# A first expert tile planned one routing round earlier, with the next round's routing set behind its first products

## The chip, the cores and the metric

The kernel runs on one core of a Trainium2 chip. The metric is the device time of one execution in microseconds (us). Engines are named as in the profile: PE (TensorE, with PEld for its weight loads), DVE (VectorE), ACT (ScalarE), POOL (GpSimd) and SP (SyncE, which here only issues transfers).

## The reference

One graph-transformer block on 12,500 nodes of 256 features, with 212,500 edges. It ends in a layer of eight experts, of which each node uses two:

```python
xn = _layernorm(x)
x = x + gat(xn, edge_index, W, a_src, a_dst) + mix(xn, w_qkv, ..., w_fc2, b_fc2)
h = _layernorm(x)
logits = h @ gate_w + gate_b
probs = softmax(logits)
top2_vals, top2_idx = top_k(probs, 2)
cw[n, top2_idx[n]] += top2_vals[n]
for e in range(8):
    out += cw[:, e:e+1] * (gelu(h @ W1[e] + b1[e]) @ W2[e] + b2[e])
x = x + out
```

`gat` is a graph attention over the edges with eight heads of 32 features, `mix` a linear attention with an MLP of 768. Everything is float32. Each expert is 256 to 512 to 256.

## The kernel before

The program runs in stages with a barrier between them: the nodes (to 205 us of the span), the edges with the mix branch beside them (to about 2,282 us), a short merge, and from about 2,298 us the experts. The change touches only the last stage.

**Two streams in the last stage.** Each engine's program there is a *routing* stream and an *expert tile* stream, woven together by `late` (L2385). Both are generators: `next` on one of them emits its instructions up to the next `yield`.

**Routing** (`route_*`, L1714 to L2047) walks over the 98 tiles of 128 nodes in 13 rounds of 8 tiles (the last has 2). A round goes, with the engine in brackets: divide the sums that the edges left and add them to x (DVE L1922 to L1933, tile `e_x`); mean and variance, tile `e_st` (DVE L216 to L1941); normalize into `e_hn`, eight activations for eight tiles (ACT L1864), and store x (ACT L1871); turn `e_hn` (PE L1817) and copy it to `e_hnt` (ACT L1882); gate product (PE L1827), copy (ACT L1887), turn back (PE L1837); softmax and the two best experts (DVE L1966 to L2006, with the exponential on ACT L1892); counts of earlier rows per expert (PE L1845, L1846); running places per expert (DVE L2012 to L2038, tile `e_row`); and then 16 scatters by POOL (L1736), two for each tile, which write the normalized rows with their node number and weights to `sorted_d` in HBM, where each expert has a region. The rounds 0, 1 and 12 scatter at once, the others during the next round. POOL also gathers the edge sums (`e_fr`, L1729) two rounds ahead, and SP loads `e_x` (L1776) two rounds ahead, at the first step of a round.

**Planning** (`plan_vector`, L2049). After a round is placed, DVE decides in 18 small instructions which new expert tiles are full: it fills `tile_row`, `expert` and `revs` for the tiles of that round and counts `planned` up. How many tiles a round plans is fixed ahead: `FULL[r]` is the number of tiles of 256 rows that are full after round r whatever the data. Before the change `FULL[0]` is set to 0, so that round 1 plans 9 tiles; `ROUND_OF[j]` is the round that plans tile j (1 for tiles 0 to 8, then 8 tiles for each round). There are 106 tiles, 97 of 256 rows and 9 of 128.

**Expert tiles** (`tile_order`, L2184). A tile j has five steps:
- `fetch` (SP L2215): waits for the plan and for all scatters up to that round, then for `x_tp` and `x_aim` of tile j-3; loads the tile's rows (`x_in`, L2226) and two biases (`x_b1c`, `x_b2c`).
- `start`: PE turns the rows (L2249), ACT copies them to `x_int` (L2286) and copies the expert's first weights to `x_w1c` (L2290); DVE takes the target rows and weights out of `x_in` (L2316 to L2319, it counts `x_aim`).
- `first`: eight products with W1 (PE L2260, 16 records in the trace), four Gelu activations (ACT L2299, the first two after half of the products).
- `second`: eight products with W2 (PE L2273, also 16 records).
- `store`: bias and weight (DVE L2328, L2332, tile `x_y`), and two scatters by POOL that add to the output (L2351).

The order is first(0), start(1), first(1), start(2), second(0), first(2), start(3), second(1) and so on, so that the products of tile j+1 cover the Gelu of tile j. An engine's instructions run in the order in which they are written. ACT needs another table for Gelu than for Exp; a table load stands before the first activation that needs it.

**What sets the weave.** `paces` (L2372) gives for each yield of the tile stream the number of routing steps that follow it. Up to the change the first of these is 350: all steps of rounds 0 and 1 and 108 of the 110 of round 2 stand before the first expert instruction, on every engine. From there 3 or 4 routing steps follow each yield, so that a round has sent its rows 12 yields before the tile stream needs them.

Of the kernel before, what the change touches and what calls it, by code (L numbers as in the profile page):

```python
# [59 lines left out]
AHEAD, NI, NW, NB = 3, 3, 4, 5  # L60
# [11 lines left out]
FULL = [max(-(-(2 * P * (f + n) - EXPERTS * (ET - 1)) // ET), 0) for f, n in zip(R_FIRST, R_TILES)]  # L72
HALF_PLACES = (2 * N_PAD + EXPERTS * (P - 1)) // P
HALVES = EXPERTS + (HALF_PLACES - EXPERTS) % 2
FULL[0], FULL[-1] = 0, (HALF_PLACES - HALVES) // 2 + HALVES
SLOTS = FULL[-1]
SUBS = [SUB] * (SLOTS - HALVES) + [1] * HALVES
LAST_FULL, LAST = SLOTS - HALVES - FULL[-2], SLOTS - FULL[-2]
# [1590 lines left out]
FIRST_ROUNDS = 2  # L1669
# [10 lines left out]
def placed(n):  # L1680

    return BOTH + LAG + 1 + n + 6
# [12 lines left out]
def at_once(r):  # L1695

    return r < FIRST_ROUNDS or r == len(ROUNDS) - 1


def round_steps(r):  # L1700
    n = R_TILES[r]
    return placed(n) + max(PLAN, 2 * n if at_once(r) else 0) + 1
# [481 lines left out]
def tile_order(first=None, start=None, second=None, store=None, fetch=None):  # L2184
    def call(step, j):
        if step:
            step(j)

    for j in range(AHEAD):
        yield ROUND_OF[j]  # L2190
        call(fetch, j)
    call(start, 0)
    for j in range(SLOTS + 1):
        now = ROUND_OF[min(j + 1, SLOTS - 1)]
        if j < SLOTS:
            call(first, j)
            yield now
        if j + 1 < SLOTS:
            call(start, j + 1)
            yield now  # L2200
        if j + AHEAD < SLOTS:
            yield ROUND_OF[j + AHEAD]
            call(fetch, j + AHEAD)
        if j:
            call(second, j - 1)
            yield now
            call(store, j - 1)
# [7 lines left out]
def experts_sync(sp, S, B):  # L2215
    def fetch(j):
        r, u, w, b = ROUND_OF[j], j % NI, j % NW, j % NB
        sp.wait_ge(S.planned, planned_by(j))
        at = sp.value_load(B.tile_row[0:1, j:j + 1], min_val=0, max_val=ZERO_ROWS)
        sp.wait_ge(S.e_z, 16 * (EXPERTS + 1) if r == len(ROUNDS) - 1 else 16)  # L2220
        for q in range(max(r - NH + 1, 0), r + 1):
            sp.wait_ge(S.e_g[q % NH], sent_to(q))
        if j >= NI:
            sp.wait_ge(S.x_tp, j - NI + 1)
            sp.wait_ge(S.x_aim, j - NI + 1)
        sp.dma_start(B.gin[u][:, 0:SUBS[j], :], B.sorted_d[bass.ds(at, SUBS[j] * P), :].rearrange("(t p) d -> p t d", p=P)).then_inc(S.x_in[u], 16)  # L2226

        ex = sp.value_load(B.expert[0:1, j:j + 1], min_val=0, max_val=EXPERTS - 1)
        if j >= NW:
            sp.wait_ge(S.x_h, HT * (j - NW + 1))  # L2230
        sp.wait_ge(S.x_b, 16)
        sp.dma_start(B.b1c[w][:, :], B.b1[:, bass.ds(ex, 1), :]).then_inc(S.x_wc[w], 16)
        if j >= NB:
            sp.wait_ge(S.x_st, 2 * (j - NB + 1))
        sp.dma_start(B.b2c[b][:, :], B.a["L0_ffn_b2"][bass.ds(ex, 1), :].to_broadcast([P, D])).then_inc(S.x_bc[b], 16)

    return tile_order(fetch=fetch)


def experts_tensor(pe, S, B):  # L2240
# [23 lines left out]
    def second(j):  # L2264
# [10 lines left out]
        t.then_inc(S.x_f2, 1)  # L2275

    return tile_order(first=first, start=start, second=second)


def experts_scalar(a, S, B):  # L2280
    def start(j):
        a.wait_ge(S.x_tp, j + 1)
        if j >= 2:
            a.wait_ge(S.x_f1, 2 * (j - 1))
        n = SUBS[j] * P
        a.activation(B.gt[j % 2][:, :, 0:n], B.banks[BANK_IN][:, :].rearrange("p (k n) -> p k n", k=KD)[:, :, 0:n], ACT.Copy).then_inc(S.x_gt, 1)  # L2286
        a.wait_ge(S.planned, planned_by(j))
        ex = a.value_load(B.expert[0:1, j:j + 1], min_val=0, max_val=EXPERTS - 1)
        a.wait_ge(S.x_w1, 16 * EXPERTS)
        a.activation(B.w1c[j % 2][:, :, :], B.w1[:, bass.ds(ex, 1), :, :].rearrange("p e k n -> p (e k) n"), ACT.Copy).then_inc(S.x_wt, 1)  # L2290

    def first(j):
        u, w, n = j % 2, j % NW, SUBS[j] * P
        a.wait_ge(S.x_wc[w], 16 * (j // NW + 1))
        if j >= 2:
            a.wait_ge(S.x_f2, j - 1)
        for m in range(HT):
            a.wait_ge(S.x_f1, 2 * j + m // 2 + 1)
            a.activation(B.ht[u][:, m, 0:n], B.banks[BANKS_H[m * 2 // HT]][:, m % 2 * ET:m % 2 * ET + n], ACT.Gelu,  # L2299
                         bias=B.b1c[w][:, m:m + 1]).then_inc(S.x_h, 1)  # L2300

    return tile_order(first=first, start=start)
# [58 lines left out]
def sent_at():  # L2361

    at, step = [], 0
    for r in range(len(ROUNDS)):
        for mark in marked(r, idle(round_steps(r))):
            step += 1
            if mark is True:
                at.append(step)
    return at


def paces():  # L2372

    sent, order = sent_at(), list(tile_order())
    due = [(0, sum(round_steps(r) for r in range(FIRST_ROUNDS + 1)))]
    due += [(order.index(r) - EARLY * (1 + (r == len(ROUNDS) - 1)), sent[r]) for r in range(FIRST_ROUNDS, len(ROUNDS))]
    counts, total = [], 0
    for t in range(len(order)):
        (t0, n0), (t1, n1) = next(((a, b) for a, b in zip(due, due[1:]) if t <= b[0]), due[-2:])
        counts.append(max(n0 - (-(n1 - n0) * (t - t0) // (t1 - t0)) - total, 0))  # L2380
        total += counts[-1]
    return counts


def late(route, tiles):  # L2385

    for _, pace in zip(tiles, paces()):
        for _ in range(pace):
            next(route, None)
    for _ in route:  # L2390
        pass
# [92 lines left out]
```

## Time and profile before

| | |
|---|---|
| median of 3 runs | 3251.28 us (3249.86 to 3253.3) |
| profiled execution, its time | 3246.55 us |
| profiled execution, its span | 3245.1 us |
| PE, PEld busy | 2637.8 us (81%), 2050.0 us (63%) |
| DVE, ACT, POOL busy | 2009.3 us (62%), 1549.6 us (48%), 2233.3 us (69%) |
| expert stage, first PE work to the end | 2325.8 to 3245 us |

The page divides the span in 40 slices of 81 us; the expert stage is the last twelve of them. In a timeline a row has the start in us, the duration in us, the engine, the line, the operation with its tiles, the number of instructions merged into it, and in square brackets how long the engine sat idle before it and which instruction's end freed it. An engine that is idle and not waited for costs nothing.

### The profile page before, as it was taken

Reading aid. Unit: us, or ns where it says so; the run is one execution under the profiler, and the core shown is the slowest. Engines: PE = TensorE matmul, PEld = TensorE weight load, DVE = VectorE, ACT = ScalarE, POOL = GpSimd, SP = SyncE. Lnnn points to the kernel's source line nnn. Section 1 sums busy time; section 2 is a strip of 40 time slices with the busy share of each in tenths; the row PEclk is TensorE's granted clock in tenths of the full one; section 3 lists DMA queues with packets and bytes.
Section 4 is the critical chain, followed back from the end, with each engine's and each line's share of the span. In section 5 each row is a group of like instructions: output and inputs, shape, how many; then the busy total and the mean of one; then the engine's idle time right before and its main releaser. Section 6 shows DMA issues by size and latency. Waiting matters only on the chain.

```text
span 3245.1 us, 42095 instructions
## 1 busy us (share of the span) xinstructions
PE 2637.8 (81%) x11512; PEld 2050.0 (63%) x11512; DVE 2009.3 (62%) x5437; ACT 1549.6 (48%) x3387; POOL 2233.3 (69%) x2193
## 2 busy tenths in 40 slices
PE   8657776888888898879888887566359999999998
PEld 6535555666566665656656666344248888788887
DVE  7445566777677676767767766687554555445422
ACT  5325543555555455546555455334234445545444
POOL 0277777777777777777777777776476667776644
PEclk9879997999999999989999999777579999999999
DMA  8797766566566666666666665665766766766653
GB/s 273 241 298 211 198 174 172 162 174 178 164 172 180 171 170 173 174 177 168 170 176 171 169 174 153 162 183 133 245 208 146 152 156 155 160 140 129 130 110 62
DMA packets 397607, 561.17 MB, mean 173 GB/s; under 512 B 71881, under 2 KB 317919, under 8 KB 397194
## 3 DMA queue, kind: packets, MB, share of 16 engines
q0 software_dynamic: 123696, 298.61, 36.3%
q1 hardware_dynamic: 196441, 170.69, 18.3%
q10 hardware_dynamic: 77161, 88.52, 10.3%
q8 instruction: 99, 1.62, 0.2%
q14 instruction: 210, 1.72, 0.2%
HBM read 402.45 MB, written 169.70 MB: 176 GB/s over the span
## 4 chain that ended last, share of the span: by engine, by line
PE 63%; DMA 11%; ACT 8%; POOL 7%; issue 6%; DVE 3%; ACTq 1%; SPq 0%; POOLq 0%; DVEq 0%
PE bank L1296 21%; PE bank L2260 10%; PE bank L2273 9%; DMA rows<-table,srcix 9%; PE bank L1095 7%; POOL rows L1232 5%; PE bank L1084 5%; PE bank L1057 2%; PE bank L605 1%; PE bank L606 1%; PE bank L865 1%; ACT L1336 1%; DMA out<-x_y,x_dest 1%; PE bank L2249 1%; PE bank L1278 1%
## 5 line engine op out<-in xcount | busy, mean ns | idle before, releaser
L1232 POOL DMA_INDIRECT rows<-table,srcix x1661 | 1597.8, 962 | 506.1 <-issue 357.4
L1296 PE MATMUL bank<-rows,onehot 128*128 128x272 f32 x3328 | 922.6, 424 | 58.3 <-ACT fout L1350 52.9
L1350 ACT ACTIVATE fout<-bank 128x272 f32<-128x272 f32 x1664 | 639.9, 397 | 573.6 <-PE bank L1296 523.9
L1296 PEld LDWEIGHTS bank<-rows,onehot 128*128 128x128 f32 x3328 | 664.0, 207 | 243.2 <-ACT fout L1350 79.3
L1442 DVE TENSOR_TENSOR rows<-rows,bank 128x1024 f32<-128x1024 f32 x416 | 484.2, 1214 | 169.0 <-ACT rows L1341 168.6
L2351 POOL DMA_INDIRECT out<-x_y,x_dest x203 | 328.1, 1616 | 230.7 <-DMA out<-x_y,x_dest 177.1
L2260 PE MATMUL bank<-x_int,x_w1c 128*128 128x256 f32 (+1 forms) x1696 | 378.9, 378 | 26.0 <-issue 22.9
L2273 PE MATMUL bank<-e_w,x_ht 128*128 x1624 | 370.5, 381 | 8.9 <-issue 6.6
L2260 PEld LDWEIGHTS bank<-x_int,x_w1c 128*128 128x128 f32 x1696 | 316.2, 194 | 77.4 <-issue 35.9
L2299 ACT ACTIVATE x_ht<-bank,x_b1c 128x256 f32<-128x256 f32 (+1 forms) x424 | 172.5, 461 | 392.3 <-PE bank L2260 392.2
L2273 PEld LDWEIGHTS bank<-e_w,x_ht 128*128 128x128 f32 x1624 | 300.4, 190 | 50.6 <-issue 14.3
L1084 PE MATMUL bank<-m_hnt,fc_w 128*128 128x512 f32 (+1 forms) x600 | 287.9, 605 | 30.2 <-ACT m_hid L1200 30.2
L2328 DVE TENSOR_TENSOR x_y<-bank,x_b2c 128x512 f32<-128x512 f32 (+1 forms) x106 | 70.8, 668 | 339.5 <-PE bank L2273 338.9
L1095 PE MATMUL bank<-fc_w,m_hid 128*128 128x256 f32 x1176 | 269.3, 380 | 0.0
L1278 PE MATMUL bank<-ident,sc_e 128*128 128x128 f32 x104 | 39.2, 377 | 272.0 <-ACT sc_e L1330 268.0
L1415 DVE SCALAR_TENSOR_TENSOR g_sdm<-notself,bank 128x128 f32<-128x128 f32 x104 | 29.9, 288 | 364.9 <-PE bank L1279 364.3
L1330 ACT ACTIVATE sc_e<-rows 128x256 f32<-128x256 f32 x104 | 43.3, 416 | 431.5 <-DMA rows<-table,srcix 412.3
L1095 PEld LDWEIGHTS bank<-fc_w,m_hid 128*128 128x128 f32 x1176 | 224.8, 191 | 33.4
L1736 POOL DMA_INDIRECT sorted_d<-e_hn,e_row x196 | 194.2, 991 | 65.0 <-issue 57.9
L1407 DVE TENSOR_TENSOR onehot<-bank,loc 128x2032 f32<-128x2032 f32 x104 | 235.8, 2267 | 0.2
L1278 PEld LDWEIGHTS bank<-ident,sc_e 128*128 128x128 f32 x104 | 16.7, 161 | 312.3 <-ACT sc_e L1330 306.9
L1084 PEld LDWEIGHTS bank<-m_hnt,fc_w 128*128 128x128 f32 x600 | 118.9, 200 | 126.7 <-issue 76.0
(404 smaller groups left out, 3244.0 us busy)
## 6 DMA issues: line engine op xcount, KB each, us to landing
frag<-fout ACTq DMA_DIRECT2D x104, 544.0 KB
rows<-table,srcix POOLq DMA_INDIRECT x1661
x_in<-sorted_d SPq DMA_DIRECT2D x97, 260.0 KB, 3.4
x_b2c<-in_L_ffn_b SPq DMA_DIRECT2D x106, 128.0 KB, 3.5
frag<-in_x ACTq DMA_DIRECT2D x1, 13416.0 KB
table<-hr SPq DMA_DIRECT2D x24, 544.0 KB, 4.0
xs<-in_x SPq DMA_DIRECT2D x24, 512.0 KB, 6.4
xg<-in_x SPq DMA_DIRECT2D x24, 512.0 KB, 6.3
```

Source lines behind the costliest of these rows:

```text
L1084: t = pe.matmul(bank[own[m % 2]][:, 0:n * P], B.mw1[:, kk, m * P:(m + 1) * P], B.m_hnt[:, kk, 0:n * P], start=(kk == 0), stop=(kk == KD - 1))
L1095: t = pe.matmul(bank[own[i // 2]][:, i % 2 * D:(i % 2 + 1) * D], B.m_hid[:, m, i * P:(i + 1) * P], B.mw2[:, m, :], start=(m == 0), stop=(m ...
L1232: p.indirect_dma_start(out=B.rows[b][:, j, :], out_offset=None, in_=B.table[:, :], in_offset=bass.IndirectOffsetOnAxis(ap=B.srcix[:, col:c ...
L1296: pe.matmul(B.banks[2 + c % 3][:, 0:ROW], B.onehot[k % 2][:, j, :], B.rows[k % NR][:, j, :], start=True, stop=True).then_inc(S.sum, 1)
L1350: a.activation(B.fout[k % 2][:, j, :], B.banks[2 + c % 3][:, 0:ROW], ACT.Copy).then_inc(S.ev, 1)
L1407: v.tensor_tensor(B.onehot[b][:, :, 0:P - 1], B.banks[0][:, 2 * P:3 * P - 1].unsqueeze(1).to_broadcast([P, CB, P - 1]), B.loc[:, k * CB:(k ...
L1442: v.tensor_tensor(h, h, w.unsqueeze(3).to_broadcast([P, n, GH, GF]), ALU.mult).then_inc(S.wgh, 1)
L1736: p.indirect_dma_start(out=B.sorted_d[:, :], out_offset=bass.IndirectOffsetOnAxis(ap=B.e_row[:, j, at:at + 1], axis=0), in_=B.e_hn[r % NH] ...
L2260: t = pe.matmul(out, B.w1c[u][:, k, m * P:(m + 1) * P], B.gt[u][:, k, 0:n], start=(k == 0), stop=(k == KD - 1))
L2273: t = pe.matmul(bk[BANKS_OUT[u]][:, i * D:(i + 1) * D], B.ht[u][:, m, i * P:(i + 1) * P], B.w2[:, bass.ds(ex * HT + m, 1), :], start=(m == ...
L2299: a.activation(B.ht[u][:, m, 0:n], B.banks[BANKS_H[m * 2 // HT]][:, m % 2 * ET:m % 2 * ET + n], ACT.Gelu, bias=B.b1c[w][:, m:m + 1]).then_ ...
L2351: p.indirect_dma_start(out=B.out[:, :], out_offset=bass.IndirectOffsetOnAxis(ap=B.dest[j % (NOUT + 1)][:, i:i + 1], axis=0), in_=B.y[j % N ...
```

## The change

Three edits in the planning of the order; no instruction's form changes except the plan's widths.

```diff
-FULL[0], FULL[-1] = 0, (HALF_PLACES - HALVES) // 2 + HALVES
+FULL[-1] = (HALF_PLACES - HALVES) // 2 + HALVES
...
-    call(start, 0)
+    if first or not store:
+        call(start, 0)
     for j in range(SLOTS + 1):
         now = ROUND_OF[min(j + 1, SLOTS - 1)]
         if j < SLOTS:
             call(first, j)
             yield now
+        if j == 0 and not (first or not store):
+            call(start, 0)
         if j + 1 < SLOTS:
             call(start, j + 1)
             yield now
...
-    due = [(0, sum(round_steps(r) for r in range(FIRST_ROUNDS + 1)))]
+    due = [(AHEAD, sum(round_steps(r) for r in range(FIRST_ROUNDS + 1)))]
...
     for t in range(len(order)):
+        if t < AHEAD:
+            counts.append(max(sent[order[t]] - total, 0))
+            total += counts[-1]
+            continue
```

`FULL[0]` is now 1: round 0 plans tile 0 (18 more DVE instructions), round 1 plans 8 tiles. The routing steps that follow the first yields were 350, 4, 3, 3 and are now 121, 121, 0, 108: SP's fetch of tile 0 stands behind round 0, its fetches of tiles 1 and 2 behind round 1, and the 108 steps of round 2 stand behind start(0) and first(0) on PE and ACT. On DVE start(0) stands behind those 108 steps. Then 4 routing steps follow each yield, until from the 17th yield on both programs have emitted the same number. Lines of the new program are up to 7 higher: 3 higher in the expert steps.

PE, from the last steps of round 1's routing on (`e_` names are routing, `x_` names the expert tile):

```order
 L1845 MATMUL bank<-e_both,e_before 128x64
 L1846 MATMUL bank<-e_both,ones 128x64
+L2252 MATMUL bank<-ident,x_in 128x128 x4
+L2263 MATMUL bank<-x_int,x_w1c 128x256 x8
 L1817 MATMUL bank<-ident,e_hn 128x128 x16
 L1827 MATMUL bank<-e_hnt,e_gw 32x256 x8
```

Tile 0's turn and first products moved ahead of round 2's routing; in the old program they stand behind its L1846.

ACT, from the end of round 1's routing to tile 1, with the new program alone:

```order
L2302 ACT_TABLE_LOAD [waits x_fc1_done]
L2302 ACTIVATE x_ht<-bank,x_b1c 128x256 [waits x_wc_in0]
L2302 ACTIVATE x_ht<-bank,x_b1c 128x256 [waits x_fc1_done] x3
L1864 ACTIVATE e_hn<-e_x,e_st 128x256 [waits e_moments]
L1864 ACTIVATE e_hn<-e_x,e_st 128x256 x7
L1871 DMA out<-e_x 128x4x256 [waits e_x1_ready]
L1871 DMA out<-e_x 128x4x256
L1882 ACTIVATE e_hnt<-bank 128x512 [waits e_hn_turned,e_gated]
L1882 ACTIVATE e_hnt<-bank 128x512 [waits e_hn_turned] x3
L1887 ACTIVATE e_lgt<-bank 128x256 [waits e_gated]
L1892 ACT_TABLE_LOAD
L1892 ACTIVATE e_pr<-e_lg 128x64 [waits e_less_max]
```

The whole of round 2's normalization and gate work stands behind tile 0's four Gelus, and round 2's exponential now has a table load before it (that load waits for nothing); tile 1's Gelu has another.

DVE, at the end of the moments of round 3:

```order
 L237 SCALAR_TENSOR_TENSOR e_st<-e_st 128x8
+L2331 TENSOR_TENSOR x_y<-bank,x_b2c 128x512
+L2335 TENSOR_TENSOR x_y<-x_y,x_scale 128x512
 L240 SCALAR_TENSOR_TENSOR e_st<-e_st 128x8
 L1941 SCALAR_TENSOR_TENSOR e_st<-e_st 128x8
-L2328 TENSOR_TENSOR x_y<-bank,x_b2c 128x512
-L2332 TENSOR_TENSOR x_y<-x_y,x_scale 128x512
```

Tile 0's store pair moved from behind the last step of round 3's moments to before its last two. On ACT all eight normalizations of round 3 now stand between start(3) and first(3), where before four stood ahead of first(2)'s Gelus and four behind them. On POOL 7, 6 and 3 scatters of round 2 stand before the stores of tiles 0, 1 and 2, where 9, 5 and 2 stood.

## Rows read from the trace of the kernel before

**Rows 1.** Windows: busy us (instructions) by engine, granted clock, DMA share, GB/s

```profile
2300.00:2390.00 90.00, 19.26 (x113) 13.83 (x113) 57.07 (x235) 20.53 (x42) 64.64 (x67) 0.56 0.86 289
...
3100.00:3170.00 70.00, 70.00 (x346) 61.70 (x345) 17.50 (x50) 29.39 (x58) 33.66 (x20) 1.00 0.50 89
```

**Rows 2.** Chain of waits from round 0's scatters to tile 0

```profile
2345.86 1.01 POOL sorted_d L1736
...
2364.88 0.96 POOL sorted_d L1736
...
2385.59 2.45 DMA sorted_d<-e_hn,e_row
...
2388.28 2.99 DMA x_in<-sorted_d
...
2391.32 1.13 PE bank L2249 x4
2394.51 3.77 PE bank L2260 x8
```

**Rows 3.** Timeline of ACT

```profile
2375.49 0.60 ACT L1864 ACTIVATE e_hn<-e_x,e_st 128x256 f32<-128x256 f32 x1 [25.23 <-DVE e_st L1941]
...
2379.44 1.05 ACT L1882 ACTIVATE e_hnt<-bank 128x512 f32<-128x512 f32 x2
...
2385.32 0.26 ACT L1892 ACTIVATE e_pr<-e_lg 128x64 f32<-128x64 f32 x1 [1.30 <-DVE e_lg L1973]
...
2399.64 1.57 ACT L2299 ACTIVATE x_ht<-bank,x_b1c 128x256 f32<-128x256 f32 x4
2401.15 0.60 ACT L2286 ACTIVATE x_int<-bank 128x512 f32<-128x512 f32 x1
...
2422.95 1.09 ACT L1882 ACTIVATE e_hnt<-bank 128x512 f32<-128x512 f32 x2
...
2442.76 1.28 ACT L1892 ACT_TABLE_LOAD   x1
2444.05 0.26 ACT L1892 ACTIVATE e_pr<-e_lg 128x64 f32<-128x64 f32 x1
```

**Rows 4.** Timeline of PE

```profile
2380.16 1.55 PE L1817 MATMUL bank<-ident,e_hn 128*128 128x128 f32 x8 [0.57 <-ACT e_hnt L1882]
...
2389.99 0.63 PE L1846 MATMUL bank<-e_both,ones 128*128 128x64 f32 x2
...
2410.39 3.62 PE L2260 MATMUL bank<-x_int,x_w1c 128*128 128x256 f32 x16
...
2425.16 3.72 PE L2273 MATMUL bank<-e_w,x_ht 128*128 x16 [0.40 <-issue]
```

**Rows 5.** Timeline of DVE

```profile
2349.18 0.23 DVE L1966 TENSOR_TENSOR e_lg<-bank,e_gb 128x64 f32<-128x64 f32 x1 [3.60 <-PE bank L1837]
...
2394.55 0.16 DVE L2057 CAST pl_ci<-pl_count 128x8 int32<-128x8 f32 x1
...
2398.22 0.22 DVE L1922 TENSOR_SCALAR e_rs<-e_fr 128x32 f32<-128x32 f32 x1
...
2411.28 0.17 DVE L1941 SCALAR_TENSOR_TENSOR e_st<-e_st 128x8 f32<-128x8 f32 x1
...
2472.99 0.69 DVE L2328 TENSOR_TENSOR x_y<-bank,x_b2c 128x512 f32<-128x512 f32 x1
```

**Rows 6.** Timeline of POOL: its waits behind tiles' stores

```profile
2413.06 1.61 POOL L2351 DMA_INDIRECT out<-x_y,x_dest  x1 [3.42 <-DVE x_y L2332]
...
2466.09 1.76 POOL L2351 DMA_INDIRECT out<-x_y,x_dest  x1 [6.17 <-DMA out<-x_y,x_dest]
```

**Rows 7.** Timeline of SP: the fetch of tile 9, the first of round 2

```profile
2445.39 0.37 SPq L2226 DMA_DIRECT2D x_in<-sorted_d  x1
```

**Rows 8.** Windows of 2 us, PE alone: busy, granted clock, DMA share, GB/s

```profile
2342.00:2344.00 2.00, 2.00 (x11) 0.50 1.08 397
...
2398.00:2400.00 2.00, 2.00 (x9) 0.94 1.09 343
```

## The prediction

> **What bounds the kernel now.** I read the page's slices first, then windows over the last stage, then the chain of waits from the first scatters to the first expert tile, then each engine's timeline from 2340 to 2480 us. The windows [rows 1] show two regimes. Up to 2390 us the stage is routing alone, PE is busy 19.26 of 90 us; late in the stage PE is busy 70 of 70. So the end is set by PE's stream of tiles, and a change at the stage's start moves the end by as much as it moves that stream once it is dense. The chain [rows 2] tells what starts it: POOL scatters round 0 and round 1 back to back, 32 scatters with the first at 2345.86; the last, started at 2385.59, lands 2.45 later, SP fetches tile 0 at 2388.28, PE turns it at 2391.32 and starts its products at 2394.51. Tile 0 waits for 16 scatters of round 1 which it would not need if round 0 alone had planned it.
>
> **Plan of round 0.** 18 DVE instructions. The same 18 of round 2 ran from 2394.55 to 2398.22, 3.67 us [rows 5]. They stand before L1966 of round 1, where DVE idled 3.60 us until 2349.18. Price 0, at most 0.1; POOL is still busy with round 0's scatters then and hides that too. Round 1's plan for 8 instead of 9 tiles costs the same.
>
> **Tile 0 goes earlier.** Its fetch now waits for the 16th scatter, started at 2364.88, not the 32nd at 2385.59: 20.71 us earlier [rows 2]. Shift all of tile 0 by that: turn at 2370.6, products at 2373.8. ACT was done with tile 0's four Gelus when it took up tile 1 at 2401.15 [rows 3]; shifted, it is free at 2380.44. SP issues the `e_x` loads of round 3 behind tile 0's fetch now, at about 2370 us, and those of round 4 behind tile 2's; DVE first reads round 3's after 2398.22 [rows 5], so this is free.
>
> **Round 2 waits for that.** ACT began round 2's normalization at 2375.49 [rows 3]; it now begins at 2380.44, 4.95 late. From there to the end of L1846 at 2389.99 + 0.63 = 2390.62 [rows 4] took 15.13. The exponential on this path gets a table load of 1.28, but the load waits for nothing and ACT idled 1.30 just there [rows 3]: price 0. So the new L1846 ends at T = 2380.44 + 15.13 = 2395.6. Bounds: if PE's clock is at its upper level throughout, the turns of 1.55 take 1.06 as those of round 3 did and the pair of count products saves as much: 1.0 less. If the second half of tile 0's products runs at half clock (3.77, as the first half did [rows 2], against 3.62 for all 16 at the full one [rows 4]), ACT is free 1.7 later. So T is 2394.6 to 2397.3. In the table load the trace speaks for itself: load at 2442.76, exponential at 2444.05, nothing else between [rows 3]. The Trainium skill (ScalarE: Activation LUTs, What ACT_TABLE_LOAD costs) gives a switch a drain of about 1.38 us beside the load's 1.28, about 2.66 in all; by it T would be some 1.4 us later and the sum 1.4 us worse. The rows show no such drain, so the sum goes by them.
>
> **Tile 1 and 2 on PE.** Their rows are in by then (fetch at 2388.28 as tile 0's before). PE turns tile 1 at T + 0.1, 3.2 later (as 2391.32 to 2394.51 [rows 2]) come its products, for 3.77 + 1.8 with a clock rising half way, then a turn of 0.5 and second(0) for 3.5: first(2) starts at T + 12.7 = 2408.3, where it started at 2410.39 [rows 4]. Here the change is 2.1 us ahead. Tile 1's Gelu pays the table load that tile 0's paid before; that is within this pattern.
>
> **Round 3 takes it back.** Round 3's moments (`e_st`) end on DVE. From round 2's counts (T, before 2390.62) to L1941 at 2411.28 took 20.66 [rows 5]. Three tiles' target steps stand in that piece before and after the change, but now tile 0's store pair stands in it too, two operations of 0.69 [rows 5], 1.3 with the gap. ACT gets `e_st` 0.2 after L1941 starts: at T + 20.66 + 1.3 + 0.2 = T + 22.2 = 2417.8. ACT's order then is eight normalizations, 3.95 (2375.49 to 2379.44), four Gelus of tile 3, 1.51 (2399.64 to 2401.15), and the copy of the turned rows [rows 3]; that copy started at 2422.95 and PE's second(2) followed at 2425.16 [rows 4], 2.2 later. So second(2) starts at T + 22.2 + 3.95 + 1.5 + 2.2 = T + 29.85 = 2425.45, **0.3 us later than before**. PE alone would be there at first(2) + 3.6 + 0.5 + 3.6 + 3.6 + 1.1 + 0.5 + 1.1 = 2422.3. PE waits 3.1 us for ACT there. From second(2) on PE, ACT and DVE stand in the same order as before, and all later work is the same.
>
> **POOL and SP.** A scatter takes POOL 1.27 (15 steps from 2345.86 to 2364.88 [rows 2]). Round 2's rows are ready when its plan starts, 3.9 after its counts (2394.55 [rows 5]), so at 2399.5; 7 scatters end at 2408.4; then POOL waits for tile 0's store pair until about 2417.0, where it went on at 2413.06 after a wait of 3.42 [rows 6]. With two scatters more behind that it is 3.9 + 2.5 = 6.5 us late, which the wait of 6.17 before 2466.09 [rows 6] and shorter ones ahead of it absorb. Round 2's last scatter has nine scatters and two stores of 2 x 1.9 in front of it from 2417.0 on and lands 2.45 later, at 2438.5, before SP fetched tile 9 at 2445.39 [rows 7]. SP's fetch of tile 3 waits for tile 0's target step on DVE, at T + 7.6 (2398.22) + 0.4, and lands 3 later, at 2406.6; its turn on PE stands behind first(2), at 2412. No price for either.
>
> **Sum.** 0 for the plan, POOL and SP, +0.3 us on PE's stream, from T's bounds -0.7 to +2.0. Against the profiled execution's time of 3246.55 that is 3246.85; that execution was 4.7 below the median of 3251.28, and I forecast the median: **3251.6 us**. A measurement of this kernel can tell about 0.2% (6.5 us) from no change; the forecast lies within.
>
> **The rivals.**
> - *Faster, PE decides.* If DVE or ACT are through with round 3 three us sooner than I say, PE's own path holds: 2.9 us ahead, 3248.4. For it: the bounds of T reach 1 us that way. Against: DVE's piece of 20.66 has no idle time that the change frees. Chance 0.12.
> - *Faster, the full tile.* Were round 2's and 3's routing hidden, the end would come by what tile 0 occupied of PE's path, from 2391.32 to 2394.51 + 3.77 + 1.8 = 2400.1 [rows 2], 8.8 us: 3242.8. It needs slack that the 4.95 at ACT denies. 0.05.
> - *Slower, the clock.* PE's granted clock was 0.50 in a window with PE busy for all of it [rows 8], and rose at 2398 before. The new program has sparse routing work on PE between tile 0 and T. If the clock stays at half through first(1), second(0) and first(2), the last two take 3.5 us more each and first(1)'s second half 1.9: 8.9, less the 3.1 that PE waits anyway, 5.8 over the sum, 3257.4; with second(1) at half too, 3260.9. It decides from 3.1 us of lost speed on. Against: the old program was as sparse before 2391 and the clock rose within tile 0. 0.08. The Trainium skill (TensorE: Matmul & The Clock Gate, HAM oscillation — how this bites in real kernels) warns of such pauses between bursts of products; the window with a busy PE at 0.50 shows that it can happen here.
> - *Slower, the drain.* If a table load at this place holds ACT for a further 1.4 us after its 1.28, T and the end move with it: 3253.0. Against: the load and the exponential stand back to back [rows 3]. 0.03. (This is the page's rule on table switches from above.)
> - *Slower, the fetch.* Tile 0's rows landed 3.0 after their issue [rows 2]; each us more is one us of T, and nothing covers it. 5 us more gives 3256.6. Against: fewer transfers are queued at 2368 than at 2391. 0.03.
> - *It does not do what it says.* The order shows tile 0 moved; only if its fetch waited for round 1 all the same would T be 2416 and PE some 20 us later: 3271. 0.01.
>
> The forecast keeps 0.68.
>
> **How the numbers follow.** Faster by over 6.5 us is the full tile and a bit of the first rival: 0.06. Slower by over 6.5 is the last case and the longer half of the clock rival, with a little of the fetch: 0.07. The rest, 0.87, is within. The range 3247 to 3257 takes in the bounds of the sum, the old runs' own spread of 3.4, the first rival, and the clock and fetch cases up to their nearer halves; it leaves out the full tile and the tails, under 0.2.
>
> **What would show it.** Right: PE L2252 of tile 0 at about 2370.6; ACT's first L1864 of round 2 at about 2380.4; L1846 at about 2395; an idle time of PE of 2 to 3 us before the turns of round 3 (L1817) or second(2), freed by ACT; L2276 of tile 2 at 2425 +- 2; POOL waiting some 8 us before its first L2354. Wrong: second(2) before 2423 (round 3's chain is not the bound), or PE dense but slow between 2396 and 2410 (the clock), or L2252 of tile 0 after 2375.

## The result, and the profile after

| | before | changed |
|---|---|---|
| median of the runs, us | 3251.28 (3249.07 to 3256.8, 5 runs) | 3267.34 (3265.05 to 3270.92, 5 runs) |
| ratio, 95% interval | | 1.0054 [1.0042, 1.0066] |
| profiled execution, us | 3246.55 | 3270.92 |
| its span, us; mean granted clock | 3245.1; 0.918 | 3269.5; 0.912 |

The changed kernel is 0.54% slower, 16 us. The forecast was no change. The profiled executions are 24.4 us apart: that of the changed kernel is the slowest of its five runs, and that of the kernel before lies 2.5 us under the fastest of the five in this table. The readings below are of those 24.4 us; that the medians' 16 are the same thing in a smaller dose is likely but not shown, since one execution of each kernel was profiled. 3.0 of the 24.4 lie ahead of the last stage: the first merge step on PE (L1505) starts at 2292.39, before at 2289.37. It starts anywhere from 2285.73 to 2293.26 in five profiles of other kernels below, whose work ahead of it is the same, so these 3.0 are not the change's. They are taken off wherever the two heads are compared.

One sentence is needed for the experiments further down: in some comparisons (sets of kernels timed one after another on one chip) the whole kernel ran 15 to 17% longer, the kernel before too (3731.6 to 3790.3 us), so a ratio is always against the kernel before in the same comparison; I call these the long comparisons.

**The head went nearly as forecast.** Timeline of PE in the changed kernel, to be read against [rows 2] and [rows 4]:

```profile
2374.23 1.11 PE L2252 MATMUL bank<-ident,x_in 128*128 128x128 f32 x4 [15.19 <-DMA x_in<-sorted_d]
...
2388.44 1.94 PE L1817 MATMUL bank<-ident,e_hn 128*128 128x128 f32 x8 [1.45 <-ACT e_hnt L1882]
2391.16 1.93 PE L1827 MATMUL bank<-e_hnt,e_gw 128*32 128x256 f32 x16 [0.78 <-ACT e_hnt L1882]
...
2399.76 0.64 PE L1846 MATMUL bank<-e_both,ones 128*128 128x64 f32 x2
...
2403.10 6.06 PE L2263 MATMUL bank<-x_int,x_w1c 128*128 128x256 f32 x16 [1.86 <-issue]
...
2412.89 3.62 PE L2263 MATMUL bank<-x_int,x_w1c 128*128 128x256 f32 x16
...
2428.56 1.94 PE L1817 MATMUL bank<-ident,e_hn 128*128 128x128 f32 x8 [2.45 <-ACT e_hnt L1882]
2430.30 1.99 PE L2276 MATMUL bank<-e_w,x_ht 128*128 x5
```

Timeline of ACT, against [rows 3]:

```profile
2383.77 4.04 ACT L1864 ACTIVATE e_hn<-e_x,e_st 128x256 f32<-128x256 f32 x8
...
2393.55 1.28 ACT L1892 ACT_TABLE_LOAD   x1
2395.09 0.26 ACT L1892 ACTIVATE e_pr<-e_lg 128x64 f32<-128x64 f32 x1 [0.25 <-DVE e_lg L1973]
...
2422.45 0.60 ACT L1864 ACTIVATE e_hn<-e_x,e_st 128x256 f32<-128x256 f32 x1 [3.64 <-DVE e_st L1941]
```

Tile 0 is turned where it was forecast (2371.2 without the 3.0; 2370.6 said), round 2's counts end at 2397.4 instead of 2395.6, and the second products of tile 2 start at 2427.3 instead of 2425.45. They stood at 2425.16 before, so PE's stream is 2.1 us late.

**The loss is behind the head.** GpSimd's timeline of the changed kernel, against [rows 6]:

```profile
2404.62 0.99 POOL L1736 DMA_INDIRECT sorted_d<-e_hn,e_row  x1 [4.25 <-DVE e_hn L2038]
...
2422.40 1.61 POOL L2354 DMA_INDIRECT out<-x_y,x_dest  x1 [8.01 <-DVE x_y L2335]
...
2461.61 1.58 POOL L2354 DMA_INDIRECT out<-x_y,x_dest  x1 [2.32 <-DMA out<-x_y,x_dest]
...
2471.35 2.38 POOL L2354 DMA_INDIRECT out<-x_y,x_dest  x1 [6.30 <-DMA out<-x_y,x_dest]
...
2478.22 1.54 POOL L2354 DMA_INDIRECT out<-x_y,x_dest  x1 [2.63 <-DMA out<-x_y,x_dest]
```

POOL stands idle for 8.01 us before tile 0's pair of output scatters, as forecast. But the wait of 6.17 that was to absorb the delay [rows 6] is still there, as 6.30, before tile 5's pair, and tile 6's scatters start at 2478.22 instead of 2466.09, 9.1 us later without the 3.0. Each of these waits is for the completion of POOL's own pair before, and the program asks for it: ahead of tile j's pair stands `p.wait_ge(S.x_y[(j - 1) % NOUT], added_to(j - 1))`. Such a wait moves along with the delay.

How far POOL lags is read by taking, for one tile, the start of VectorE's bias addition and of the tile's first output scatter. Timelines of DVE and POOL for tile 57 and tile 105 (the last), kernel before:

```profile
2894.80 0.69 DVE L2328 TENSOR_TENSOR x_y<-bank,x_b2c 128x512 f32<-128x512 f32 x1 [4.81 <-PE bank L2273]
2915.70 1.60 POOL L2351 DMA_INDIRECT out<-x_y,x_dest  x1 [0.30 <-issue]
...
3234.94 0.42 DVE L2328 TENSOR_TENSOR x_y<-bank,x_b2c 128x256 f32<-128x256 f32 x1 [0.84 <-PE bank L2273]
3242.20 1.54 POOL L2351 DMA_INDIRECT out<-x_y,x_dest  x1 [1.43 <-DMA out<-x_y,x_dest]
```

The same in the changed kernel:

```profile
2902.15 0.69 DVE L2331 TENSOR_TENSOR x_y<-bank,x_b2c 128x512 f32<-128x512 f32 x1 [1.90 <-PE bank L2276]
2936.15 1.60 POOL L2354 DMA_INDIRECT out<-x_y,x_dest  x1 [0.30 <-issue]
...
3250.00 0.42 DVE L2331 TENSOR_TENSOR x_y<-bank,x_b2c 128x256 f32<-128x256 f32 x1 [2.36 <-DMA out<-x_y,x_dest]
3266.55 1.54 POOL L2354 DMA_INDIRECT out<-x_y,x_dest  x1 [1.43 <-DMA out<-x_y,x_dest]
```

The lag at tile 6, 57 and 105 is 4.4, 20.9 and 7.3 us before, and 10.6, 34.0 and 16.5 in the changed kernel. It goes up and down in both (before it is 10.9 us at tile 9, 2.6 at tile 15, 20.9 at tile 57 and 5.7 at tile 70), but what the changed kernel has more is not worked off: 6.2 us at tile 6, 13.1 at tile 57, 18.0 at tile 70, 9.2 at the end. Windows and waits from 2430 us on, kernel before (busy us of PE, PEld, DVE, ACT and POOL; then engine, line, releaser: us in total, times, longest):

```profile
2430.00:3245.00 815.00, 773.26 (x3932) 662.94 (x3930) 370.52 (x1451) 392.56 (x750) 524.88 (x405) 0.99 0.64 134
...
POOL out L2351 <- DMA out<-x_y,x_dest: 177.1, 57, 6.8
POOL sorted_d L1736 <- issue: 43.9, 144, 0.3
POOL out L2351 <- issue: 42.1, 138, 0.3
POOL e_fr L1729 <- issue: 17.1, 56, 0.3
POOL out L2351 <- DVE x_y L2332: 3.7, 3, 3.1
POOL out L2351 <- DVE x_y L2328: 3.5, 1, 3.5
...
SPq L2222 <- DMA sorted_d<-e_hn,e_row: 18.7, 6, 5.3
```

Changed kernel:

```profile
POOL out L2354 <- DMA out<-x_y,x_dest: 188.2, 58, 6.3
...
DVE x_dest L2319 <- DMA out<-x_y,x_dest: 45.8, 17, 5.8
...
SPq L2225 <- DMA sorted_d<-e_hn,e_row: 99.0, 9, 20.8
```

In the kernel before POOL is busy for 524.9 of these 815 us, spends 103.1 on issuing, waits 177.1 for its own scatters and 7.2, in four waits, for VectorE. That is 812.3 in all: POOL is a second bound, beside PE. Its lag reaches others at two places. VectorE's target step of tile j waits for the output scatters of tile j - 7 (`if j > NOUT`, NOUT = 6): no such wait before, 17 of them now. And SP's fetch of a round's first tile waits for that round's scatters of rows, which stand on POOL behind the late output scatters: 99.0 us instead of 18.7. Windows of the changed kernel late in the stage:

```profile
3060.00:3170.00 110.00, 106.55 (x520) 93.02 (x519) 35.97 (x134) 47.03 (x88) 58.76 (x41) 1.00 0.63 123
3170.00:3269.00 99.00, 74.86 (x423) 65.26 (x421) 21.47 (x71) 37.14 (x82) 46.20 (x29) 0.91 0.38 59
```

PE, busy 70 of 70 there before [rows 1], has gaps now. Two of them end with a late fetch, on PE's timeline:

```profile
3080.93 0.66 PE L2252 MATMUL bank<-ident,x_in 128*128 128x128 f32 x4 [0.72 <-DMA x_in<-sorted_d]
...
3098.62 0.66 PE L2252 MATMUL bank<-ident,x_in 128*128 128x128 f32 x4 [2.31 <-DMA x_in<-sorted_d]
```

The 24.4 us are: 3.0 ahead of the stage; 2.9 on VectorE's tiles up to tile 45 (5.3 to 5.9 with the 3.0); 9.2 more up to tile 105 (its addition is 15.1 late); and 9.3 because the last scatter lags by 16.5 instead of 7.3. The 9.3 are POOL's. Of the 9.2 the trace ties 5.0 to POOL's lag directly, as waits of PE that the kernel before has not: 3.0 for fetched rows and 2.0 for VectorE. They come where VectorE waits for output scatters (first at tile 51), but what became of the rest was not followed.

### The profile page after: what moved, and what is told of

Read it like the earlier page. It is cut to its first block, busy times and chain, and to the rows that moved or that the text cites. A ratio compares the mean times of both kernels' runs of the same rounds, so it can differ in the third digit from the quotient of the medians.

```text
span 3269.5 us, 42116 instructions
## 1 busy us (share of the span) xinstructions
PE 2655.0 (81%) x11512; PEld 2059.1 (63%) x11512; DVE 2013.9 (62%) x5455; ACT 1554.4 (48%) x3389; POOL 2240.1 (69%) x2193
## 4 chain that ended last, share of the span: by engine, by line
PE 55%; POOL 12%; DMA 12%; issue 9%; ACT 8%; DVE 3%; ACTq 1%; SPq 0%; POOLq 0%; DVEq 0%
PE bank L1296 22%; DMA rows<-table,srcix 8%; PE bank L1095 7%; PE bank L2263 6%; PE bank L2276 5%; POOL rows L1232 5%; PE bank L1084 5%; POOL out L2354 4%; POOL sorted_d L1736 2%; PE bank L1057 2%; PE bank L605 1%; PE bank L606 1%; DMA out<-x_y,x_dest 1%; PE bank L865 1%; ACT L1336 1%
## 5 line engine op out<-in xcount | busy, mean ns | idle before, releaser
L1296 PE MATMUL bank<-rows,onehot 128*128 128x272 f32 x3328 | 934.2, 428 | 59.2 <-ACT fout L1350 51.3
L1296 PEld LDWEIGHTS bank<-rows,onehot 128*128 128x128 f32 x3328 | 671.2, 209 | 247.5 <-ACT fout L1350 76.9
L1278 PEld LDWEIGHTS bank<-ident,sc_e 128*128 128x128 f32 x104 | 16.6, 160 | 310.2 <-ACT sc_e L1330 298.6
```

The costliest lines, as they stand in the source:

```text
L1296: pe.matmul(B.banks[2 + c % 3][:, 0:ROW], B.onehot[k % 2][:, j, :], B.rows[k % NR][:, j, :], start=True, stop=True).then_inc(S.sum, 1)
```

## The experiments

Theory A: GpSimd's lag makes the loss. Theory B: it is without effect, and PE's late stream, the fetches or the clock make it. Each kernel had runs of the kernel before beside it, in the same comparison.

**The plan alone.** In the kernel before:

```diff
-FULL[0], FULL[-1] = 0, (HALF_PLACES - HALVES) // 2 + HALVES
+FULL[-1] = (HALF_PLACES - HALVES) // 2 + HALVES
```

> The kernel before with round 0's full tile planned by round 0 (18 small VectorE instructions more, round 1 plans 8 tiles instead of 9) and no other part of the change: every queue but VectorE's stays as it was. All theories: the same as the kernel before within its own spread, 3249 to 3254 us; the prediction took this part as hidden in an idle of 3.60 us. If it is 3260 or more, the cost of the change lies in the plan and not in the order, and both theories below fall.

Measured: 3246.76 us against 3247.4, 0.9997 [0.9986, 1.0008]. The plan costs nothing; the loss is in the order.

**GpSimd's sends first.** In the changed kernel, GpSimd's program alone:

```diff
-    late(route_pool(p, S, B), experts_pool(p, S, B))
+    late(route_pool(p, S, B), experts_pool(p, S, B), sends_first(paces(), AHEAD, 400))
```

`late` takes these counts in place of its own, and

```diff
+def sends_first(counts, t, upto):
+
+    more = max(upto - sum(counts[:t + 1]), 0)
+    counts[t] += more
+    for i in range(t + 1, len(counts)):
+        less = min(more, counts[i])
+        counts[i], more = counts[i] - less, more - less
+    return counts
```

brings the routing steps that stand ahead of tile 0's output pair up to 400, and takes them from the places behind it.

> The changed kernel with GpSimd's queue alone written in another order: all 16 scatters of round 2's rows stand before tile 0's pair of output scatters (7, 6 and 3 of them stood before the pairs of tiles 0, 1 and 2); TensorE's, VectorE's and ScalarE's order is that of the changed kernel. Theory A (GpSimd's queue is full from 2430 us on, and the change makes it start about 6.5 us later, of which 8.0 us is idle time before tile 0's output scatters): the idle time is filled by 9 scatters that had to be sent anyway, the lag of the output scatters behind VectorE falls by some 8 us from tile 2 on, and the run takes 3251 to 3257 us. Theory B (the products' chain starts late and the clock or the fetches do the rest, GpSimd's lag is without effect): no difference, 3264 to 3270 us.

Measured: 3248.12 us, 1.0003 [0.9992, 1.0015]: the loss of the first comparison (1.0054) is not there, and the time lies under the 3251 to 3257 us that theory A had expected, though the lag falls by less than its 8 us: by 3.5 at tile 2 and 6.0 at tile 6. The changed kernel itself was not timed beside it. Timelines of DVE and POOL for tiles 57 and 105 in this kernel:

```profile
2897.99 0.69 DVE L2331 TENSOR_TENSOR x_y<-bank,x_b2c 128x512 f32<-128x512 f32 x1 [4.42 <-PE bank L2276]
2925.46 1.61 POOL L2354 DMA_INDIRECT out<-x_y,x_dest  x1 [0.30 <-issue]
...
3238.39 0.42 DVE L2331 TENSOR_TENSOR x_y<-bank,x_b2c 128x256 f32<-128x256 f32 x1 [0.84 <-PE bank L2276]
3242.49 1.54 POOL L2354 DMA_INDIRECT out<-x_y,x_dest  x1 [1.42 <-DMA out<-x_y,x_dest]
```

PE, ACT, DVE and SP are in the changed kernel's order, the first merge step starts at 2292.80 (2292.39 there), and VectorE adds tile 6's bias at 2467.62 (2467.59). Only the lag differs: 4.6 instead of 10.6 at tile 6, 27.5 instead of 34.0 at tile 57, 4.1 instead of 16.5 at the end, with no wait of VectorE on an output scatter. The last scatter starts 24.1 us earlier. Tile 105's addition is 3.5 us after that of the kernel before, but the merge had started 3.4 later too. Counted from each profile's own start of the merge, VectorE's additions are 2.5 us late at tiles 3 to 9 here and 0.4 early at tile 20, where the changed kernel is still 2.9 late: PE's late head is at most 2.9 us of the loss. A lag of 27.5 us did no harm and one of 34.0 did, so its price seems to set in at a threshold between them. The lags themselves vary by some us from profile to profile: the kernel with the plan alone, with POOL's order of the kernel before, has 24.7 at tile 57 and 3.9 at the end where that has 20.9 and 7.3.

**A short delay.** In the kernel before, ahead of tile 0's pair:

```diff
+        if j == 0:
+            for k in range(64):
+                p.memset(B.pad[:, 2 * k:2 * k + 2], 0.0)
```

> The kernel before with 64 memsets of 128x2 added on GpSimd, once, ahead of tile 0's output scatters: by the 0.10 us that a memset of 128x1 takes in its profile some 6.5 us of pure delay of that queue at 2420 us, and nothing else changed on any engine. Theory A: the lag is never worked off, because GpSimd's round takes as long as TensorE's; the output scatters run 6 us and more later to the end, and the run takes 3257 to 3267 us. Theory B: the lag is absorbed within some tiles, 3249 to 3254 us.

Measured: 3247.39 us, 0.9997 [0.9986, 1.0007]. It tells little, since the delay was not 6.5 us: the lag was 2.2 us more than in the kernel before at tile 0 and 0.3 more at tile 6, so the few waits on VectorE took up that much. The 64 memsets overlapped:

```profile
2410.34 1.95 POOL L2350 MEMSET pad<- 128x2 f32 x64 [4.43 <-DVE x_y L2333]
```

**The gathers apart.** In the kernel before, GpSimd's routing alone:

```diff
-            if part == 0:
-                if k < late:
+            m, rest = divmod(step - SPREAD * late, 6 if late else SPREAD)
+            if k < late:
+                if part == 0:
...
-                elif r >= 2 and r + 2 < len(ROUNDS) and k < late + R_TILES[r + 2]:
-                    fetch(r + 2, k - late)
+            elif rest == 0 and r >= 2 and r + 2 < len(ROUNDS) and m < R_TILES[r + 2]:
+                fetch(r + 2, m)
```

> The kernel before with GpSimd's queue alone changed: from round 2 on the gathers of a round (2, 5 and 1 of them between output pairs, then three pairs with nothing between) are spread as 1, 3, 2 and 2, so that one place with pairs back to back is left instead of two; same instructions, same number. Theory A: in each round one or two waits on the completion of the pair before (2 to 6 us each) get hidden behind gathers, GpSimd's waits on output scatters fall from 177 us by 20 or more, its lag at the end (7 to 28 us) falls under 5 us, and the run takes 3243 to 3250 us. Theory B: GpSimd's waits don't matter, 3249 to 3254 us.

Measured: 3245.76 us, 0.9996 [0.9986, 1.0006]. POOL's waits in this kernel, from 2430 us:

```profile
POOL out L2352 <- DMA out<-x_y,x_dest: 99.9, 31, 6.4
POOL out L2352 <- DVE x_y L2333: 78.1, 23, 6.3
```

The waits on its own scatters fall from 177.1 us to 99.9, and 78.1 us of real slack appear, waits on VectorE. The lag peaks at 12.0. Yet the time is that of the kernel before: I had expected some us of gain. That fits a threshold: with the old order the lag does not reach the point where it costs, and a margin is gained, not time.

**True delays.** Again the kernel before, now with memsets of 128x256 that wait for one another, 18 or 36 of them:

```diff
+        if j == 0:
+            for k in range(36):
+                p.memset(B.pad[:, :], 0.0).then_inc(S.e_const, 1)
+                p.wait_ge(S.e_const, E_CONSTS + k + 1)
```

Beside them ran the changed kernel once more and the changed kernel with the gathers apart.

> The kernel before with 18 memsets of 128x256 on GpSimd behind VectorE's signal for tile 0, each waiting for the one before (about 0.35 us each by the 0.31 us row of its profile), some 6.5 us in all, once; nothing else is changed. Theory A, as it stands after the first four runs (the lag of the output scatters behind VectorE is carried on, grows to a peak at tiles 57 to 59, and costs nothing until it passes the seven tiles for which buffers exist; that point lies between the 27.5 us of the kernel with the sends first, which ran like the kernel before, and the 34.0 us of the changed kernel): peak lag 26 to 29 us at tile 57, few or no waits of VectorE on output scatters, 3247 to 3253 us. Theory A in its first form (every us of lag stays to the end): 3254 us or more. Theory B (the lag is worked off and has no part in it): lag at tile 57 as in the kernel before (20.9), 3246 to 3249 us.

> The same with 36 memsets, some 13 us. Theory A with a threshold: peak lag 33 us or more at tile 57, VectorE waits for output scatters 10 to 20 times (17 times, 45.8 us in the changed kernel, none in the one before), fetches behind the last rounds' scatters are late, and the run takes 3256 to 3268 us, though TensorE's, VectorE's and ScalarE's order is wholly that of the kernel before. Theory B: 3246 to 3250 us.

> The changed kernel itself, on the chip and beside the runs of the kernel before that the other kernels of this call have. Theory A and B: a ratio of 1.0054 as in the first comparison (3262 to 3270 us). If it is within 0.2% of the kernel before here, the loss belongs to the chip or to the moment and not to the order alone.

> The changed kernel with the gathers of each round spread on GpSimd's queue between the output pairs (1, 3, 2 and 2 in place of 2, 5, 1 and none), all else the changed kernel's; GpSimd's first 60 us are left as they are, so the late start stays. Theory A: the lag doesn't grow from round to round (in the kernel before the same edit brought the lag at tile 57 from 20.9 to 10.6 us), it peaks under 20 us, VectorE never waits for an output scatter, and the run takes 3246 to 3252 us. Theory B: no difference to the changed kernel, 3262 to 3270 us.

This was a long comparison (kernel before 3731.55 us). Ratios: 18 memsets 1.0013 [0.9992, 1.0034], 36 memsets 1.0012 [0.9992, 1.0033], changed kernel 1.0011 [0.9991, 1.0031], with the gathers apart 0.9994 [0.9969, 1.0018]. None of the four can be told from the kernel before. The four were measured again, with a theory C beside A: that the first comparison's loss was one chip's.

> The changed kernel once more. In the call before, the chip ran everything 15% slower (the kernel before 3731.6 us; eight tiles of the product stage took some 75 us and more there instead of 70), GpSimd's queue had idle time of its own (133 us of waits on VectorE) and the change was worth +0.11% [-0.09, +0.31]. Theory A: where the kernel before takes 3250 us, GpSimd's round is as long as TensorE's and the ratio is 1.004 to 1.006 (3260 to 3270 us); on a chip as slow as the last one it is 1.000 to 1.002. Theory C (new: the first comparison's +16 us was one chip's): within 0.2% of the kernel before here too.

> The kernel before with 36 chained memsets (on the chip before: 14.5 us) on GpSimd ahead of tile 0's output scatters, where nothing else is changed. Theory A, on a chip where the kernel before takes 3250 us: the lag at tile 57 is 33 us or more, VectorE waits on output scatters 10 times or more, and the run takes 3256 to 3268 us. Theory C, or the lag without effect: 3246 to 3251 us.

> The same with 18 memsets (7.5 us on the chip before). Theory A on a fast chip: between the kernel before and the one with 36; lag at tile 57 of 26 to 30 us, 3247 to 3256 us. Theory C: 3246 to 3250 us.

> The changed kernel with each round's gathers spread between the output pairs of GpSimd's queue. Theory A on a fast chip: the lag peaks under 20 us, VectorE never waits for an output scatter, 3246 to 3252 us, faster than the changed kernel by 10 us or more. Theory C: the same time as the changed kernel beside it.

Another long comparison (3783.75): changed kernel 1.0019 [1.0002, 1.0036], 36 memsets 1.0038 [1.0016, 1.006], 18 memsets 1.0026 [1.0008, 1.0044], gathers apart 0.9987 [0.9966, 1.0009]. The changed kernel's waits in that comparison show why theory A has nothing to work on there; POOL from 2895 us on:

```profile
POOL out L2354 <- DVE x_y L2335: 155.3, 36, 10.4
POOL out L2354 <- DMA out<-x_y,x_dest: 82.2, 24, 6.0
```

PE is busy for less of the time here, 63.20 and 60.92 us in two windows of 70, so its round takes longer:

```profile
2965.00:3035.00 70.00, 63.20 (x306) 53.44 (x307) 34.78 (x136) 33.72 (x62) 45.80 (x38) 0.95 0.63 143
3035.00:3105.00 70.00, 60.92 (x299) 51.39 (x298) 34.17 (x138) 28.36 (x52) 43.25 (x35) 0.93 0.58 123
```

POOL waits 155 us for VectorE, and the lag of tile 57 is 9.4 us in place of 34.0. Even after 36 memsets it is back to 2.6 us at tile 21. Three kernels were measured once more, then the delay alone:

> The changed kernel beside the kernel before for a fourth time, since both calls before fell on chips that ran everything 15 and 16% slower (lag of the output scatters at tile 57 of 9.4 to 11.4 us there, no wait of VectorE on a scatter, ratios 1.0011 and 1.0019). Theory A: where the kernel before takes 3250 us, the lag at tile 57 is 30 us or more, VectorE waits for output scatters 10 times or more, and the ratio is 1.004 to 1.006. Theory C (the first +16 us were one chip's): 1.000 to 1.002, whatever the chip.

> The kernel before with some 13.5 us of chained memsets on GpSimd ahead of tile 0's output scatters and nothing else changed. Theory A, where the kernel before takes 3250 us: lag at tile 57 of 33 us or more, 10 or more waits of VectorE on output scatters, 3256 to 3268 us. Lag without effect: 3246 to 3251 us. On a slow chip: 1.001 to 1.004, as in the two calls before.

> The changed kernel with each round's gathers spread between the output pairs of GpSimd's queue. Theory A, where the kernel before takes 3250 us: lag at tile 57 of 10 to 20 us, no wait of VectorE on a scatter, 3246 to 3252 us. Theory C: the same time as the changed kernel beside it.

> The kernel before with some 13.5 us of chained memsets on GpSimd ahead of tile 0's output scatters, sent alone for another chip. Theory A, where the kernel before takes 3250 us: lag at tile 57 of 33 us or more, 10 or more waits of VectorE on output scatters, 3256 to 3268 us. Lag without effect: 3246 to 3251 us. Where the kernel before takes over 3700 us: a ratio of 1.001 to 1.004 with a lag under 12 us at tile 57, as in the three calls before.

All in long comparisons: changed kernel 1.003 [1.0007, 1.0054], 36 memsets 1.0023 [1.0003, 1.0044], gathers apart 0.9992 [0.9963, 1.002] (kernel before 3785.21), and the 36 memsets alone 1.0014 [0.9998, 1.0031] (3784.42).

> The kernel before with some 13.5 us of chained memsets on GpSimd ahead of tile 0's output scatters, once more, for a chip on which the kernel before takes 3250 us. Theory A there: lag at tile 57 of 33 us or more, 10 or more waits of VectorE on output scatters, 3256 to 3268 us. Lag without effect: 3246 to 3251 us. Where the kernel before takes over 3700 us: a ratio of 1.001 to 1.004, lag under 12 us at tile 57.

Here the kernel before took 3244.99 us (12 runs): **3263.54 us, 1.0047 [1.0027, 1.0066]**. PE, ACT, DVE and SP are wholly in the old order, and the loss is about that of the change. The time lies in the 3256 to 3268 us of theory A, and the profile, of an execution of 3263.2 us, has each of its signs. The delay, on POOL's timeline:

```profile
2416.67 13.21 POOL L2350 MEMSET pad<- 128x256 f32 x36 [3.20 <-DVE x_y L2333]
```

Waits of DVE and SP from 2430 us:

```profile
DVE x_dest L2317 <- DMA out<-x_y,x_dest: 68.5, 24, 5.3
...
SPq L2223 <- DMA sorted_d<-e_hn,e_row: 143.2, 10, 24.0
```

Tile 57 and tile 105:

```profile
2901.66 0.69 DVE L2329 TENSOR_TENSOR x_y<-bank,x_b2c 128x512 f32<-128x512 f32 x1
2936.65 1.60 POOL L2356 DMA_INDIRECT out<-x_y,x_dest  x1 [0.30 <-issue]
...
3243.39 0.42 DVE L2329 TENSOR_TENSOR x_y<-bank,x_b2c 128x256 f32<-128x256 f32 x1 [0.84 <-PE bank L2274]
3258.93 1.54 POOL L2356 DMA_INDIRECT out<-x_y,x_dest  x1 [1.43 <-DMA out<-x_y,x_dest]
```

The lag is 35.0 us at tile 57 and 15.5 at the end, with 24 waits of VectorE. VectorE's addition is 0.8 us behind that of the kernel before at tile 45 and 9.5 at tile 55: the time is lost where the lag is at its height, not where the delay stands. Of the seven runs five took 3263 to 3267 us, one 3254.31 and one 3246.48, the time of the kernel before. This scatter fits a threshold, with a lag at its edge that costs all or nothing; the lag of the two shorter executions is not known, so this is not shown. It takes 13.5 us of delay to do what 6.2 us more at tile 6 do in the changed kernel, because the lag does not grow so much afterwards here (17.9 at tile 6, 35.0 at tile 57).

> The changed kernel with each round's gathers spread between the output pairs of GpSimd's queue, right behind a call that met a chip on which the kernel before takes 3245 us (and the delayed kernel 3263.5). Theory A, if this chip is such a one: lag at tile 57 of 10 to 20 us in place of 34.0, no wait of VectorE on an output scatter, a ratio of 0.998 to 1.001 in place of 1.0054. If the changed kernel's loss has another cause than the grown lag: 1.004 to 1.006. On a slow chip: 0.999 to 1.000 as in the three calls before.

A long comparison again (3790.33): 1.0 [0.9979, 1.002]. So the second cure was never measured in a comparison where the loss shows in full.

**What stays open.** The changed kernel's 16 us stand on one comparison: all its repeats fell into long ones, so theory C is weakened by the delay alone (1.0047 on another kernel) and not refuted on the changed kernel. Whether the gathers apart cure it, and what 18 memsets cost, in a comparison that is not a long one, was not measured. How much of the loss goes by VectorE's target waits and how much by SP's late fetches was not separated. And why, in the long comparisons, the changed kernel (1.0011, 1.0019, 1.003) and the delays (1.0012 to 1.0038) still cost 0.1 to 0.4%, though the lag is worked off within twenty tiles and VectorE never waits: a fetch that is late once in the head would do it, but I have not shown it. There the changed kernel with the gathers apart had a shorter median than the changed kernel beside it each time (by 5 to 14 us three times), which points at POOL's order, though no interval was taken for that difference. No version beat the kernel before: the best ratios, 0.9996 and 0.9997, are no difference.

## Why the prediction was wrong

- *Plan of round 0, price 0*: right (plan alone 0.9997).
- *Tile 0 goes earlier*: right, 2371.2 against 2370.6.
- *Round 2 waits for that, T = 2395.6*: 2397.4, a hair over the upper bound of 2397.3. ACT began as said (2380.8 against 2380.44); from there to the end of the counts it took 16.6 us instead of 15.13. 1.25 of the 1.5 are PE's clock: the second half of the turns took 1.94 us where it took 1.55, and the gate products 1.93 where they took 1.07, at a granted clock of 0.50 (the lower level, 1.2 GHz) against 0.71 and 1.00. The bounds had let the clock in this piece only rise and not fall. The table load behaved as the rows said: the load at 2393.55, the exponential at 2395.09, 0.26 us behind its end and freed by VectorE. The further 1.38 of drain that the Trainium skill states (ScalarE: Activation LUTs, What ACT_TABLE_LOAD costs) is not seen here either.
- *The clock*: tile 1's first products took 6.06 us for 16 where 5.57 was forecast, tile 2's ran at full clock (3.62). The rival as it was put, half clock up to first(2), did not occur; the clock cost 0.5 here and the 1.25 above.
- *Round 3 takes it back, second(2) at +0.3*: +2.1. PE waits 2.45 and 0.73 for ACT there, 3.1 forecast. The term was too small by the 1.8 us that T was late; the mechanism was right. The kernel with the sends first has it too, and runs like the kernel before.
- **The POOL step, the one that failed**: "6.5 us late, which the wait of 6.17 before 2466.09 and shorter ones ahead of it absorb". The idle time of 8 us was forecast and is there (8.01). But a wait absorbs a delay only if what it waits for does not move with it. The row named its releaser, the DMA of POOL's own last output scatter [rows 6]; the only waits that absorb are those on VectorE, and of these POOL had 7.2 us in 815. Price taken: 0. Price measured: about 16 us (1.0054 for the changed kernel, 1.0003 for the same with the sends first, each against the kernel before in its own comparison).
- *"From second(2) on all later work is the same"*: so it was on PE, ACT and DVE, but the queue beside them was at its own limit. [Rows 1] show PE at 70 of 70 at 3100 us, and I took that for the end's only bound. POOL is busy for 49 of 70 us in the rounds from 2555 to 2835 us, which looks like slack and is not, since 0.3 us of issue before each of some 40 transfers and 8 to 12 us of waits on completions fill the rest.
- *The rivals*: none of them was this one. The slower ones were about the clock, a drain, a fetch and a tile 0 that had not moved, each priced in the head.

## What to carry to other kernels

Before a delay on a queue is called absorbed, look at who ends the waits that are to absorb it: a wait on the queue's own transfer moves with it, and only a wait on another engine is slack. Add busy time, issue time and such waits of each queue over one round of a loop; if they fill the round, the queue is a bound whatever its busy share says, and it keeps what it loses beyond its few waits on others. How many buffers stand between it and its neighbours then decides when the loss shows, so the same few us of delay can cost nothing or, as here, some 16 us.

## What the runs showed of the hardware that I had not expected

- The same chip ran the kernel before in 3731.6 us in one comparison and in 3245.0 in another, about an hour later; the mean granted clock of the profiled runs was 0.88 and 0.91. In the long comparisons PE's busy share in the stage is lower (61 to 63 of 70 us instead of 66), and POOL's bound vanishes with it. What makes them long is not known.
- An output scatter mostly occupies POOL for 1.5 to 1.6 us, but it lands 3.9 to 7.9 us after its issue (changed kernel, up to 2500 us): a pair that the program makes wait for the pair before stood for up to 6.8 us. Where five gathers stand between, the wait is gone (0.30 of issue alone).
- 64 independent memsets of 128x2 took 1.95 us in all, though each is 106 ns long in the trace: they overlap. 36 of 128x256 that wait for one another took 13.21, 0.37 each.
